# Selective-scan block with routed experts on one core: ScalarE makes five of sixteen scan inputs, by two transposes on TensorE

## The reference

```python
def step(h, inp):
    u_t, d_t, B_t, C_t = inp
    dA = jnp.exp(d_t[..., None] * As)
    h = h * dA + (d_t * u_t)[..., None] * B_t[:, :, None, :]
    y = jnp.einsum('bkcn,bkn->bkc', h, C_t)
    return (h, y)
```

## Time and profile before

| what | value |
|---|---|
| median of 3 runs | 2063.02 us (2061.94 to 2063.2) |
| profiled execution, its own time | 2065.29 us |
| span in the profile | 2063.5 us |
| DVE busy | 1645.3 us, 80% |
| PE busy | 1512.7 us, 73% |
| POOL busy | 1437.9 us, 70% |
| ACT busy | 852.7 us, 41% |
| mean granted TensorE clock | 0.857 of full |
| scan stage, pair 0 | about 177 to 786 us |
| scan stage, pair 1 | about 1027 to 1624 us |

### The profile page before, as it was taken

The page is one execution under the profiler, slowest core; times in us unless marked ns, Lnnn a source line. Parts: engine busy times, 40 slices in busy tenths (PEclk is TensorE's granted clock), DMA queues, the critical chain, the costliest instruction groups (busy, mean ns, idle before and its releaser), DMA issues.

```text
span 2063.5 us, 14513 instructions
## 1 busy us (share of the span) xinstructions
PE 1512.7 (73%) x3788; PEld 673.2 (33%) x3789; DVE 1645.3 (80%) x1640; ACT 852.7 (41%) x1288; POOL 1437.9 (70%) x535
## 2 busy tenths in 40 slices
PE   5754677776677776877377677677677676999997
PEld 2221222232232232622122233233232253555554
DVE  6699999997999997677999999999999674232232
ACT  3673544544545443257354445545454320111110
POOL 2497999997999994045799999999999412222231
PEclk9866888888888888788588888888898877999999
DMA  3156345346344331202834354344433383111110
GB/s 110 41 199 220 111 147 163 115 139 199 108 146 140 113 106 61 85 31 77 305 111 141 123 155 145 114 139 151 131 126 107 114 287 116 43 42 49 48 48 19
DMA packets 120145, 248.92 MB, mean 121 GB/s; under 512 B 20863, under 2 KB 33698, under 8 KB 116241
## 3 DMA queue, kind: packets, MB, share of 16 engines
q1 hardware_dynamic: 114960, 234.00, 34.2%
q0 software_dynamic: 5120, 14.21, 2.2%
HBM read 205.10 MB, written 44.60 MB: 121 GB/s over the span
## 4 chain that ended last, share of the span: by engine, by line
DVE 42%; PE 24%; POOL 11%; issue 8%; DMA 7%; SPq 4%; ACT 2%; POOLq 0%; DVEq 0%
DVE arena L849 20%; PE psum L1226 9%; POOL arena L457 9%; DVE arena L836 8%; DMA arena<-bc_dram 7%; PE psum L1245 5%; DVE arena L796 3%; SPq L328 3%; DVE arena L816 3%; DVE arena L814 2%; PE psum L1124 2%; POOL arena L442 1%; PE psum L1086 1%; DVE arena L810 1%; PE psum L1154 1%
## 5 line engine op out<-in xcount | busy, mean ns | idle before, releaser
L1124 PE MATMUL psum<-arena,ident 128*128 128x512 f32 x1536 | 815.5, 685 | 332.8 <-POOL arena L457 332.6
L457 POOL TENSOR_TENSOR arena<-arena 128x1536 f32<-128x1536 f32 x256 | 875.0, 3439 | 74.4 <-DMA arena<-bc_dram 38.2
L849 DVE TENSOR_TENSOR_SCAN arena<-psum,arena 128x512 f32<-128x512 f32 x768 | 899.3, 1238 | 14.5 <-ACT psum L645 14.4
L645 ACT ACTIVATE psum<-arena 128x512 f32<-128x512 f32 x768 | 528.4, 691 | 628.7 <-DVE arena L849 628.7
L1124 PEld LDWEIGHTS psum<-arena,ident 128*128 128x128 f32 x1536 | 323.1, 218 | 823.1 <-POOL arena L457 460.0
L836 DVE TENSOR_TENSOR arena<-psum,arena 128x1536 f32<-128x1536 f32 x176 | 306.3, 1741 | 25.4 <-issue 19.8
L442 POOL TENSOR_TENSOR arena<-arena 128x1536 f32<-128x1536 f32 x80 | 275.1, 3439 | 0.0
L1226 PE MATMUL psum<-arena 128*128 x480 | 203.8, 562 | 0.0
L494 POOL TENSOR_TENSOR gap<-one 128x1 f32<-128x1 f32 x40 | 11.4, 284 | 212.0 <-DVE arena L1013 212.0
L719 ACT ACTIVATE arena<-psum 128x384 f32<-128x384 f32 x40 | 19.6, 490 | 301.6 <-PE psum L1217 301.6
L418 POOL TENSOR_TENSOR arena<-arena 128x1024 f32<-128x1024 f32 x16 | 50.0, 3126 | 108.4 <-ACT arena L557 106.4
(11 more groups left out here) (149 smaller groups left out, 1261.0 us busy)
## 6 DMA issues: line engine op xcount, KB each, us to landing
arena<-bc_dram SPq DMA_DIRECT2D x1024, 128.0 KB, 3.0
step_dram<-arena SPq DMA_DIRECT2D x16, 1536.0 KB, 6.3
arena<-step_dram SPq DMA_DIRECT2D x32, 768.0 KB, 7.7
arena<-in_x SPq DMA_DIRECT2D x8, 1536.0 KB, 9.7
arena<-in_w SPq DMA_DIRECT2D x6, 1876.0 KB, 10.5
t_dram<-arena SPq DMA_DIRECT2D x16, 386.0 KB, 4.0
arena<-in_w SPq DMA_DIRECT2D x4, 1536.0 KB, 14.4
z_dram<-arena SPq DMA_DIRECT2D x2, 1536.0 KB, 5.4
```

What stands on the lines that cost most here:

```text
L457: g.tensor_tensor(x, x, Cs[c % C_RING][:, None, :].to_broadcast([P, CG, HALF]), ALU.mult)\
L645: a.activation(dA[e % 2], steps[g % 2][0][:, j, :], ACT.Exp, scale=A[:, KORDER[kk], j, n:n + 1]).then_inc(s_dA, 1)
L849: v.tensor_tensor_scan(x, dA[(CG * c + j) % 2][:, ::way], x, 0.0 if first else state[:, n, j:j + 1], ALU.mult, ALU.add)\
L1124: ins = pe.matmul(bank[j], ident[:, :], X3[c % RING][:, j, :], start=False, stop=(n == NS - 1), skip_group_check=True)
```

## The change

`MAKER` says who makes the input of each n: P is GpSimd (n = 0, 4, 8, 12), D is VectorE (1, 3, 5, 7, 9, 11, 13), A is ScalarE with TensorE (2, 6, 10, 14, 15). For an A step, TensorE transposes du once a group into PSUM (`transpose_du`: 12 transposes 128x128, in the bank of `dups`), and ScalarE copies it to SBUF (`duT_out`). In that layout positions lie on partitions, so a row of B is a column, and a scale that each partition reads from `BT` applies it: ScalarE makes 8 blocks of 128x192 for one input (`scale_duT`), and TensorE transposes them back, four 128x128 for each j, into the slots `dA[e % 2]`. The exponentials of an A step go to SBUF instead (`dAs`), and the scan reads its input from PSUM and writes the ring slot. `SCALED` sets at which n how many blocks are made, for which step. `LAG` delays `add_up` by three steps on TensorE. `BT` is made in the preparation (`b_columns`).

The SBUF for this lies where the images of pair 1 used to arrive, so `load_x` moves behind the last scan, `norm_stats` behind `times_z`, and `norm_std` with it.

```diff
-BY_GPSIMD = (1, 4, 7, 10, 13)
+MAKER = "PDADPDADPDADPDAA"
+BY_SCALAR = (2, 6, 10, 14, 15)
+LAST_D = 13
+SCALED = {15: ((2, 0, 3),), 0: ((2, 3, 8),), 3: ((6, 0, 3),), 4: ((6, 3, 8),), 6: ((10, 0, 5),),
+          8: ((10, 5, 8), (14, 0, 2)), 10: ((14, 2, 7),), 11: ((14, 7, 8),), 12: ((15, 0, 5),), 13: ((15, 5, 8),)}
+LAG = 3
+B_AHEAD = 5
...
                     if s == 4 * NS and p + 1 < PAIRS:
-                        load_x(p + 1)
+                        sp.dma_start(win, w_in).then_inc(s_win, 16)
 
                 sp.wait_ge(s_scan, CG * STEPS * (p + 1))
+                if p + 1 < PAIRS:
+                    load_x(p + 1)
...
-                    if 0 < i < ND - 1:
-                        xd_out(i + 1)
+                    if i < ND - 1:
+                        b_columns(i)
...
-                    if i == 0:
-                        xd_out(1)
+                    if i < ND - 1:
+                        xd_out(i + 1)
...
+                def duT_out(g):
+                    a.wait_ge(s_duTps, GROUPS_OF_PAIR * p + g + 1)
+                    a.wait_ge(s_scaled, 2 * LB * inputs_before(STEPS * p + g * NS, "A"))
+                    a.activation(duT.rearrange("p (j l) -> p j l", j=CG), dups, ACT.Copy).then_inc(s_duT, 1)
+
+                def scale_duT(s, first, last):
...
+                    for t in range(first, last):
+                        k, b = t // 2, t % 2
+                        a.activation(blocks(scaled[index % 2])[:, :, k, b, :], blocks(duT)[:, :, k, b, :], ACT.Copy,
+                                     scale=BT[:, kk, LB * half + k, b, BY_SCALAR.index(n):BY_SCALAR.index(n) + 1])\
+                         .then_inc(s_scaled, 1)
...
                 def exp(s, j):
                     kk, g, _, n, _ = place(s)
-                    e = CG * (STEPS * p + s) + j
+                    c = STEPS * p + s
+                    e = CG * c + j
+                    if MAKER[n] == "A":
+                        if inputs_before(c, "A"):
+                            last = max(q for q in range(c) if MAKER[q % NS] == "A")
+                            a.wait_ge(s_scan, CG * last + j + 1)
+                        a.activation(dAs[j], steps[g % 2][0][:, j, :], ACT.Exp,
+                                     scale=A[:, KORDER[kk], j, n:n + 1]).then_inc(s_dAs, 1)
+                        return
...
                 a.wait_ge(s_vread, CG * ND * (p + 1))
                 a.wait_ge(s_dst[0], 16 * (2 * p + 2))
+                a.wait_ge(s_relu, CG * ND * (p + 1))
                 for s in range(STEPS):
...
                     exp(s, 0)
                     exp(s, 1)
+                    if s == 0:
+                        duT_out(0)
+                        du_to_psum(0)
+                        scale_duT(BY_SCALAR[0], 0, 3)
...
                     exp(s, 2)
                     if n == 2 and g:
                         y_out(g - 1)
+                    for m, f, l in todo:
+                        if m < STEPS:
+                            scale_duT(m, f, l)
+                    if n == NS - 2 and g + 1 < GROUPS_OF_PAIR:
+                        duT_out(g + 1)
...
+                def transpose_input(s):
+                    c = STEPS * p + s
+                    index = inputs_before(c, "A")
+                    pe.wait_ge(s_scaled, 2 * LB * (index + 1))
+                    for j in range(CG):
+                        e = CG * c + j
+                        pe.wait_ge(s_scan, e - 1)
+                        for k in range(LB):
+                            at = (j * LB + k) * P
+                            ins = pe.transpose(dA[e % 2][:, k * P:(k + 1) * P], scaled[index % 2][:, at:at + P],
+                                               ident[:, :])
+                        ins.then_inc(s_inT, 1)
+
+                transpose_du(0)
+                added = 0
                 for s in range(STEPS):
-                    add_up(s)
+                    n, g = s % NS, s // NS
+                    if MAKER[n] == "A":
+                        transpose_input(s)
+                    if not (MAKER[n] == "A" and MAKER[(n + 1) % NS] == "A"):
+                        while added <= s - LAG:
+                            add_up(added)
+                            added += 1
+                    if n == LAST_D and g + 1 < GROUPS_OF_PAIR:
+                        transpose_du(g + 1)
```

More of the change, by code:

```diff
@@ L143, in build @@
         E = [arena[:, b * GL:(b + 1) * GL] for b in range(2)]
+        duT = arena[:, 0:CG * HALF]
+        scaled = [arena[:, (1 + u) * CG * HALF:(2 + u) * CG * HALF] for u in range(2)]
+        blocks = lambda ap: ap.rearrange("p (j t b c) -> p j t b c", j=CG, t=LB, b=2)
+        dAs = [arena[:, 3 * CG * HALF + j * HALF:3 * CG * HALF + (j + 1) * HALF] for j in range(CG)]
         one_e = arena[:, ring_at:ring_at + GL]
@@ L693, in _ @@
                      .then_inc(s_std2, 1)
-                if p + 1 < PAIRS:
-                    for b in range(2):
-                        norm_std(p + 1, b)
                 for h in range(2):
@@ L702, in _ @@
                                      scale=lng[:, j:j + 1]).then_inc(s_yg, 1)
+                if p + 1 < PAIRS:
+                    for b in range(2):
+                        norm_std(p + 1, b)
                 for g in range(GROUPS + 1):
@@ L1081, in xd_rows @@
                         pe.wait_ge(s_xd, 2 * c)
+                        pe.wait_ge(s_bt, c)
                     for h in range(2):
@@ L1088, in xd_rows, with b_columns @@
                         ins.then_inc(s_xdps, 1)
+                def b_columns(i):
+                    c = ND * p + i
+                    pe.wait_ge(s_xd, 2 * c + 2)
+                    for q in range(TT):
+                        ins = pe.transpose(bank[0][:, q * 64:(q + 1) * 64], xd[i % 2][64:128, q * P:(q + 1) * P],
+                                           ident[64:128, 64:128])
+                    ins.then_inc(s_btps, 1)
                 xd_rows(0)
```

123 lines of the change are left out of this document (83 added, 40 removed).

## The result

The changed kernel takes **2095.03 us** (median of 4 runs, 2094.77 to 2095.64), the kernel before 2063.11 (4 runs, 2061.94 to 2064.32): ratio 1.0155, 95% interval 1.0137 to 1.0173. It is 1.5% slower. Predicted were 2102 us, 1.9% slower.

What follows compares the result with a forecast made beforehand. VectorE was taken to bound the kernel; 105.6 us saved on inputs against added delays, mostly waits for ScalarE, summed to +39 us, 2102 us in the median's terms. The range was 2055 to 2150 us, the likeliest case 2075 to 2125.

Steps and rivals of the forecast that it cites:

- (a): Five scaled blocks at n = 0, 4, 8, 12 delay the next step's exponentials and so VectorE: +63 us.
- (b): Three scaled blocks at n = 13, in front of the exponential of n = 14, delay VectorE: +5 us.
- (c): Hand-over of du: ScalarE's two copies in front of the exponentials of n = 15 delay VectorE: +18 us.
- (g): Between the pairs, the statistics now stand in the open behind `times_z`: +6 us.
- (j): At the end of a pair, five add_ups behind the last transposes make y_out later: +9 us.
- (d): y_out at n = 2 waits for the late add_up of step 15, exponentials and VectorE behind it: +49 us.
- (f): VectorE's waits for late rows of B in the scans shrink from 19.8 us to 4: -16 us.
- (e): Transposes into the slots come 0.23 us late at half clock, taken for a share of 0.2: +5 us.
- Faster by the price of a block: Rival: block pitch below 0.28 together with a full clock makes the kernel faster, to 2039 us; chance 0.12.
- Clean gain: Rival: ScalarE can run ahead in the scans, so its predicted delays vanish, 1962 us; chance 0.04.
- The clock stays low: Rival: TensorE's clock stays low in the scans, giving 2125 to 2190 us; chance 0.16.
- TensorE as a second bound: Rival: at a mixed clock, add_ups between A steps cost 0 to 2 us a group, 2102 to 2134; chance 0.13.

Runs made afterwards that it cites:

- e5: Changed kernel with a constant 1.0 in place of the scale per partition in the scaled blocks; 2073.09 us, ratio 1.0027.
- e2: Changed kernel with `SCALED` spread out: no blocks at n = 0, 4, 8, 13, two at n = 12; 2042.63 us, ratio 0.9894.
- e3: Changed kernel with du copied to PSUM behind the last exponential of n = 15, not before its first; 2086.96 us, ratio 1.0112.
- e8: e7 with pair 1's statistics moved, half behind the last scan, half in front of the first `scale`; 1995.41 us, ratio 0.9659.
- e11: Changed kernel with rows of B asked for four steps ahead, as before the change; 2096.02 us, ratio 1.0145.
- e12: e10 with the input of n = 12 made by VectorE instead of GpSimd; 2029.35 us, ratio 0.9818.
- e1: Changed kernel with y_out one step later, at n = 3 instead of n = 2; 2074.11 us, ratio 1.0048.
- e4: Changed kernel with the edits of e1, e2 and e3 together, two of step 2's blocks at n = 0; 2004.89 us, ratio 0.9711.
- e7: e4 with `LAG` = 2 and y_out back at n = 2; 1999.44 us, ratio 0.9668.
- e9: e8 with a delay of three steps at n = 13 only, `LAG` = 2 elsewhere; 1998.57 us, ratio 0.9674.
- e10: e9 with `keep_state` in front of the second exponential of the next step; 1993.87 us, ratio 0.9644.

## Why the prediction came out as it did

**The mechanism was right, and so were most sizes.** It said that VectorE would give back more in waits for ScalarE than 64 inputs save. (a), the term that decides the sign, was 63 and measured 62: the price of a block, taken from the exponential's row and a width, was 0.34 and is 0.345. e5 changes nothing but this price and the wait follows it within 0.01 us; e2 takes the blocks out of the chain and the wait is 0. (b) and (c) are within 1.5 us of their forecasts and the stretches with (g) to (j) within 1. e3 takes the wait of (c) from 17.1 to 1.8, and e8 shortens the stretch of (g) by 5.4.

**The term that was mis-sized is (d), 49 for 38.** Its mechanism held: from the start of the scans of n = 2 to y_out it is 4.5 to 4.6 us in all 14 groups, predicted 4.7 at full clock, and it was 1.9 before. But I added 10 us for one y_out in four at half clock, and each of the 14 cost 2.70 more than before, where 2.76 was for the full clock. The same place in group 1 has a granted clock of 1.00 in add_up of step 15 and behind it (windows of the changed kernel, columns as above), and this add_up takes 2.74 us in all 14 groups:

```profile
263.50:266.30 2.80, 2.77 (x8) 0.98 (x6) 1.82 (x2) 0.00 (x0) 2.80 (x2) 1.00 0.23 83
267.80:270.60 2.80, 2.79 (x7) 1.36 (x8) 2.13 (x2) 1.96 (x4) 2.71 (x1) 1.00 0.97 336
```

The mean of a stage, 0.85 or 0.87, doesn't say how the clock stands at one place in it, and the kernel before couldn't have told it either. There the same add_up took 4.3 to 5.5 us in all 14 groups, in group 1 with a granted clock of 0.53 (255.0 to 260.3):

```profile
255.00 5.31 PE L1124 MATMUL psum<-arena,ident 128*128 128x512 f32 x6 [3.94 <-POOL arena L457]
```

The share of one in four was a guess. This add_up is below the full clock 0 times of 14 in the changed kernel, 2 times in e2 and 5 times in e3, which differ from it only in what ScalarE does when; and each time costs 1.3 to 1.7 us, not the 2.6 of an add_up at half clock throughout.

**(f) was 5 too small, (e) 4 too small.** In (e), 0.2 of 29 is 6 and not 5. All late rows of B disappeared, where I let 4 us stand. I had put a share of it on the earlier request, which e11 takes away without an effect.

**The signs.** VectorE's waits in front of scans are about 68 us a pair, forecast 75. The list gives 54 of them to L701. The rest stands under L696 and L1235, because in front of n = 14 and 15 the exponentials are those into SBUF, which the prediction didn't tell apart.

**The rivals.** Faster by the price of a block: refuted, by 0.345 against the 0.28 from which it would decide. Clean gain: the waits are there. The clock stays low: it didn't. The stages had 0.87 with some 1130 more transposes, those before 0.85 and 0.86, and the add_up in front of y_out ran at the full clock. The Trainium skill (TensorE: Matmul & The Clock Gate, Part 4: PE-mode transpose) says that transposes don't count as busy in the same way. The rows go both ways on it: in the earlier trace rows the clock rose during transposes, in e12 it was 0.50 in those of n = 15 and 0.92 in the add_ups behind them (last rows below). TensorE as a second bound was not decisive in the changed kernel (12.7 us of waits), but e1, e4, e7, e9 and e12 show that it is next: as soon as ScalarE's chains are out of the way, 18 to 39 us of waits for transposes stand at n = 6, 14 or 2, wherever the order of add_ups and transposes is tightest. I saw it as a matter of the clock. In e1 it is that; in e12 it is five add_ups in the place of four.

**What the change is worth.** With its work ordered otherwise and nothing else, it is 3.3 to 3.6% faster than the kernel before (e8 to e10), where as written it is 1.5% slower. The kernel before was not reordered in the same way: its own 14.4 us of waits behind y_out, 0.7%, might have gone too, so that part of the gain may not be the change's. In e10 VectorE still waits 46 us in the scan stages, of the 106 that the inputs cost.

**Open:** what of the 20 us of (f) is the images and what the fewer rows; what would be won by A steps that are evenly apart; and what decides the clock at the add_up of step 15.

## What to carry to other kernels

Work moved to an idle engine is free only if it doesn't stand between a result that the busy engine has just released and the next one that it needs: with two buffers, write down the chain (here 1.31 + 0.63 + X + 0.69 + 0.13), see how much X it allows (0.78), and put every new instruction where VectorE does something else. A delay constant in an in-order engine's program is part of that chain: of what is delayed, look who waits for the last one of a group. And when a wait is removed, expect it at the next place where the order is tight: e7 and e9 moved as much as they removed, e1 and e3 lost a third and a half of theirs to matmuls at a lower clock, and e2 a quarter, most of it to the place that it gave three of its blocks. An engine busy for 97% of a stage (GpSimd in e10) was still not what held it.

## What the runs showed of the hardware

- A scan that reads its input from PSUM and its factor from SBUF takes 1.234 us, one that does the reverse 1.232.
- ScalarE, 128x192 SBUF to SBUF, fp32: 0.439 us alone and 0.345 in a row with a scale per partition; 0.25 in a row with a constant. The pointer costs 0.095 an instruction, in a row too.
- The length of a pause alone didn't tell TensorE's clock. It was 1.00 behind 1.54 us of idling and 0.63 behind 2.84 (the changed kernel, 267.80 and 500.00 to 504.60) and 0.50 behind 3.58 (e1), but 1.00 again behind 3.76 in e4 (timeline, then a window):

```profile
1500.90 2.84 PE L1199 MATMUL psum<-arena,ident 128*128 128x512 f32 x6 [3.76 <-ACT arena L722]
1500.95:1503.70 2.75, 2.75 (x7) 1.31 (x8) 2.65 (x3) 1.69 (x3) 2.75 (x2) 1.00 0.00 0
```

- In e12 the clock was 0.50 in the transposes of n = 15 and 0.92 in the five add_ups behind them (windows, columns as above):

```profile
460.00:462.30 2.30, 2.14 (x9) 1.75 (x10) 2.28 (x2) 2.30 (x3) 2.30 (x1) 0.50 0.35 96
462.30:476.40 14.10, 14.10 (x32) 6.07 (x32) 11.48 (x10) 10.21 (x24) 13.98 (x5) 0.92 0.43 117
```
